# Cross-attention without key projections: queries taken through the transposed key weights, scored on the context in blocks of 125 rows

## The chip, the cores and the metric

The kernel runs on 1 core of one Trainium2 chip. The metric is the device time of one execution in microseconds, as the median of several runs.

## The reference, cut to what matters

`x` is (8, 100, 512), the context (8, 361, 512), all float32. A single-head attention adds 0.1 of its result to `x`. After it come two layers of 16-head cross-attention (128 columns a head) with a layer norm ahead of each, and an MLP (512 to 2048 to 512) with its own norm.

```python
qh = (q_in @ wq + bq).reshape(b, q_len, H, K)
kh = (kv_in @ wk + bk).reshape(b, t, H, K)
vh = (kv_in @ wv + bv).reshape(b, t, H, K)
kh = jnp.concatenate([kh, jnp.broadcast_to(bias_k, (b, 1, H, K))], axis=1)
vh = jnp.concatenate([vh, jnp.broadcast_to(bias_v, (b, 1, H, K))], axis=1)
logits = jnp.einsum('bqhk,bthk->bhqt', qh, kh) / scale
weights = jax.nn.softmax(logits, axis=-1)
ctx = jnp.einsum('bhqt,bthk->bqhk', weights, vh).reshape(b, q_len, H * K)
return ctx @ wo + bo
```

## The kernel before

**Precision.** Nearly every float32 matrix is held as a high part and a low part, the rest after rounding. A product is three matmuls (high by high, high by low, low by high; `mm3`, lines L466 to L468), and over 512 contracted rows (`product`) twelve. ScalarE makes the high part of each result out of PSUM, VectorE the low part behind it (`low` L978, `low_biased` L982), so that each result goes TensorE, ScalarE, VectorE and back.

**Stages.** The single-head stage (`single_head` on each engine) handles the 8 batches in two turns of four. Its VectorE order is in `batches`, and `residual` (L1047) ends a turn. Then, for each half of the batches (4 batches, 400 query rows), come two layers and the MLP, in loops of the program (`Fori`). `x_ready` is raised at the end of each block: by the `flag` memset (L986) after the single head and after each layer, by the copy of `x_next` (L1288) after an MLP. I call one layer on one half a pass; there are four. A normalisation begins each pass and each MLP (`norm_sums`, `norm_act`, `norm_dve`); it needs `norm_p`, which SP loads as its first act after `x_ready`.

**A pass** goes over 8 pairs of heads, 8 steps a pair, one for each batch and head (`pair_steps`). A step projects the keys of one head and batch (`keys`, 12 matmuls of 362 columns: the 361 context rows and one column for `bias_k`), scores 100 queries on them (`scores_at`, 3 matmuls), takes the softmax (`maxima`, `exps`, `normalise`), transposes the probabilities (`prob_rows`, L594) and, every second step, attends for both heads at once over the context rows (`attend`, 36 matmuls of 200 columns). The values' weights are applied after the attention (`outputs_part`, with L624 for the biases), then the output weights (`project`). Two key projections run inside the normalisation:

```python
norm_sums(half * 6 + l * 2, lambda: keys(0, 0, True))
keys(0, 1, True)
pe.wait_ge(n_lo, half * 6 + l * 2 + 2)
```

**Weights** come by SP in pieces of 512 KB (two heads of one kind, `load`, L259) into two stage buffers, and GpSimd splits them (`split_one`: copy L339, subtraction L361, for each head).

## Time and profile before

| | us |
|---|---|
| median of 3 runs | 2142.31 (2141.86 to 2143.52) |
| span of the profiled execution | 2136.5 |
| median less this span | 5.8 |
| TensorE busy | 1999.7 (94%) |
| VectorE busy | 1478.8 (69%) |
| ScalarE busy | 765.9 (36%) |
| GpSimd busy | 746.6 (35%) |

The profiled execution has no time of its own beside its span; the span is from its first to its last instruction. Busy time is the union of an engine's instructions. Matmuls overlap in the records, so the pace of a row of them is read from the difference of two starts, not from the length of one.

### The profile page before, as it was taken

What the parts mean: (1) busy time and instruction counts of PE and PEld (TensorE: products, weight loads), DVE (VectorE), ACT (ScalarE), POOL (GpSimd) and SP (SyncE); (2) the same over time, 40 slices, a digit from 0 to 9 for tenths busy, and PEclk for the clock granted to TensorE, in tenths of its full rate; (3) what the DMA queues carried; (4) which work ended last, traced back from release to release, by engine and by line L of the source; (5) the groups of instructions that cost most, each with busy time, mean ns of one, the idle gap of its engine ahead of it and who ended that gap; (6) DMA issues with size and microseconds to landing.
All of it is one profiled execution on the core that took longest, in us unless ns stands there. A gap on an engine that the chain in (4) does not pass through costs nothing.

```text
span 2136.5 us, 38048 instructions
## 1 busy us (share of the span) xinstructions
PE 1999.7 (94%) x13128; PEld 1944.5 (91%) x13128; DVE 1478.8 (69%) x3365; ACT 765.9 (36%) x1723; POOL 746.6 (35%) x609
## 2 busy tenths in 40 slices
PE   7779999999889999999797999999979999999978
PEld 4679999999879999999696999999979999999968
DVE  3456777777567777777667677777766777777677
ACT  3433333333233333333453333333333333333354
POOL 2223333333313333333361333333323333333355
PEclk9999999999999999999898999999989999999989
DMA  7401111111001111111432011111101111111054
GB/s 222 137 20 51 40 39 39 39 39 40 21 31 40 39 39 39 41 49 38 140 117 74 31 40 39 39 39 41 47 23 40 47 42 39 39 39 40 21 170 130
DMA packets 37685, 119.84 MB, mean 56 GB/s; under 512 B 5168, under 2 KB 6320, under 8 KB 37600
## 3 DMA queue, kind: packets, MB, share of 16 engines
q1 hardware_dynamic: 35296, 114.52, 16.6%
q10 hardware_dynamic: 2304, 4.20, 0.6%
q8 instruction: 52, 0.85, 0.2%
q14 instruction: 33, 0.27, 0.0%
HBM read 116.24 MB, written 2.46 MB: 56 GB/s over the span
## 4 chain that ended last, share of the span: by engine, by line
PE 84%; DVE 7%; issue 4%; ACT 3%; DMA 1%; POOL 1%; SPq 0%; DVEq 0%; ACTq 0%; POOLq 0%
PE psum L466 26%; PE psum L467 26%; PE psum L468 26%; PE psum L594 3%; PE psum L482 1%; DMA cr_stage<-ctx_dram 1%; DVE rstd L1096 1%; DVE prob L998 1%; PE psum L624 1%; DVE xT L1178 1%; DVE stats L990 1%; DVE xT L1276 0%; DVE cen L1100 0%; DVE u_lo L978 0%; DVE pT_lo L978 0%
## 5 line engine op out<-in xcount | busy, mean ns | idle before, releaser
L466 PE MATMUL psum<-pT_hi,ctx_rows_hi 121*128 121x200 f32 (+1 forms) x1536 | 425.1, 277 | 15.4 <-DVE pT_lo L978 10.5
L467 PE MATMUL psum<-pT_lo,ctx_rows_hi 121*128 121x200 f32 (+1 forms) x1536 | 426.3, 278 | 0.0
L468 PE MATMUL psum<-pT_hi,ctx_rows_lo 121*128 121x200 f32 (+1 forms) x1536 | 424.4, 276 | 0.0
L855 ACT ACTIVATE prob<-psum,stats 100x362 f32<-100x362 f32 x256 | 144.4, 564 | 631.8 <-DVE stats L992 631.8
L466 PE MATMUL psum<-ctxT_hi,wk_hi 128*128 128x362 f32 x1024 | 336.9, 329 | 0.0
L467 PE MATMUL psum<-ctxT_lo,wk_hi 128*128 128x362 f32 x1024 | 335.5, 328 | 0.0
L468 PE MATMUL psum<-ctxT_hi,wk_lo 128*128 128x362 f32 x1024 | 335.5, 328 | 0.0
L339 POOL TENSOR_TENSOR wo_hi<-stage,zero_col 128x512 fp32r<-128x512 f32 x60 | 62.4, 1041 | 770.0 <-PE psum L468 660.3
L466 PEld LDWEIGHTS psum<-pT_hi,ctx_rows_hi 121*128 121x128 f32 (+1 forms) x1536 | 297.3, 194 | 24.5 <-issue 12.0
L468 PEld LDWEIGHTS psum<-pT_hi,ctx_rows_lo 121*128 121x128 f32 (+1 forms) x1536 | 298.2, 194 | 0.0
L467 PEld LDWEIGHTS psum<-pT_lo,ctx_rows_hi 121*128 121x128 f32 (+1 forms) x1536 | 296.0, 193 | 0.0
L978 DVE TENSOR_TENSOR u_lo<-psum,u_hi 128x400 fp32r<-128x400 f32 x256 | 141.6, 572 | 103.2 <-ACT u_hi L738 102.2
L466 PEld LDWEIGHTS psum<-ctxT_hi,wk_hi 128*128 128x128 f32 x1024 | 193.3, 189 | 0.6
L467 PEld LDWEIGHTS psum<-ctxT_lo,wk_hi 128*128 128x128 f32 x1024 | 193.0, 189 | 0.0
L468 PEld LDWEIGHTS psum<-ctxT_hi,wk_lo 128*128 128x128 f32 x1024 | 192.8, 188 | 0.0
L738 ACT ACTIVATE u_hi<-psum 128x400 fp32r<-128x400 f32 x256 | 126.1, 504 | 164.7 <-PE psum L468 164.7
L996 DVE RECIPROCAL stats<-stats 100x1 f32<-100x1 f32 x264 | 43.3, 164 | 190.2 <-ACT prob L855 184.4
L738 ACT ACTIVATE pT_hi<-psum 121x300 fp32r<-121x300 f32 x256 | 106.9, 418 | 177.2 <-PE psum L594 176.7
L978 DVE TENSOR_TENSOR pT_lo<-psum,pT_hi 121x300 fp32r<-121x300 f32 x256 | 117.9, 460 | 67.1 <-ACT pT_hi L738 67.1
L998 DVE TENSOR_SCALAR prob<-prob,stats 100x362 f32<-100x362 f32 (+1 forms) x264 | 153.7, 582 | 9.2
L982 DVE SCALAR_TENSOR_TENSOR k_lo<-psum,bk_c,k_hi 128x361 fp32r<-128x361 f32 x256 | 150.2, 587 | 3.0 <-ACT k_hi L844 0.7
L990 DVE TENSOR_REDUCE stats<-psum 100x1 f32<-100x362 f32 (+1 forms) x264 | 139.7, 529 | 12.8 <-PE psum L468 8.9
(176 smaller groups left out, 4687.2 us busy)
## 6 DMA issues: line engine op xcount, KB each, us to landing
stage<-pair_w_dram SPq DMA_DIRECT2D x130, 512.0 KB, 3.7
stage<-mlp_w_dram SPq DMA_DIRECT2D x32, 512.0 KB, 3.7
ct_stage<-ctxT_dram SPq DMA_DIRECT2D x16, 722.0 KB, 4.4
cr_stage<-ctx_dram SPq DMA_DIRECT2D x32, 240.0 KB
l0w<-l_w_dram ACTq DMA_DIRECT2D x16, 256.0 KB, 12.9
cr_stage<-ctx_dram SPq DMA_DIRECT2D x16, 242.0 KB
x_next<-out_dram SPq DMA_DIRECT2D x2, 800.0 KB, 5.6
out_dram<-y_out SPq DMA_DIRECT2D x8, 200.0 KB, 2.0
```

Of the source, the lines that this page charges most:

```text
L339: return nc.gpsimd.tensor_tensor(out, in_, zero_col[0:in_.shape[0], :].broadcast_to(tuple(in_.shape)), ALU.add)
L466: pe.matmul(out, w_hi, x_hi, start=start, stop=False)
L467: pe.matmul(out, w_hi, x_lo, start=False, stop=False)
L468: return pe.matmul(out, w_lo, x_hi, start=False, stop=stop)
L594: mm = pe.transpose(bank[PT_BANK][0:rows, t * L:(t + 1) * L], prob[0:L, t0:t0 + rows], ident[0:L, 0:L])
L738: return nc.scalar.activation(out, in_, ACT.Copy)
L855: nc.scalar.activation(prob[0:L, :], bank[S_BANK][0:L, 0:T], ACT.Exp, bias=stat[:, 1:2], scale=HEAD_SCALE, accum_out=stat[:, 2:3]).then_in ...
L978: return nc.vector.tensor_tensor(out, value, hi.bitcast(F32), sub)
L982: return nc.vector.scalar_tensor_tensor(out=out, in0=value, scalar=bias, in1=hi.bitcast(F32), op0=ALU.add, op1=sub)
L990: nc.vector.reduce_max(st[:, 0:1], scores, AX_X).then_inc(max_s, 1)
L996: nc.vector.reciprocal(st[:, 3:4], st[:, 2:3]).then_inc(rcp_s, 1)
L998: nc.vector.tensor_scalar(p, p, st[:, 3:4], None, ALU.mult).then_inc(norm_s, 1)
```

## The change

- There are no projected keys. A head's query result goes through the head's transposed key weights (`through_keys`, 4 results of 3 matmuls, 400 columns), which gives 512 numbers for each query, and these are scored on the split context itself (`scores`, 12 matmuls of 362 columns for one block and batch). The key bias cancels in the softmax except against the `bias_k` column. That column's scores come from a product of their own at the start of a pass (16 rows, 400 columns), go to DRAM and come back as columns (`s0_d`, three reads of 4 numbers a run), and VectorE copies one column into the scores before the maximum.
- The weights of that product are made at run time: for each of the 32 heads of both layers a 0.5 KB row is spread over 128 partitions and a 256 KB piece of `wq` is loaded (`load_key_weights`), GpSimd multiplies (`key_weights`), VectorE sums (`key_sums`). VectorE does 24 of the 32 sums inside turn 1 of the single head, six after each batch, and 8 after its last residual; then come two more operations and `x_ready`.
- All 16 heads of a batch form one row of 1600 queries, cut in 12 blocks of 125 and one of 100. Two blocks are attended together (250 columns, `attend`), the last three together (350 columns). A step is such a group on one batch: 24 steps a pass, 52 blocks in place of 64.
- The order of queries, key products, values and outputs is the table `PIECES`; they share three PSUM banks in turn (`RBUFS`). Queries and their products live in a ring of five heads (`a`).
- Weights come one head at a time (256 KB) through two stage buffers to four weight buffers. SP issues the first six of a pass ahead of `norm_p`.
- The loops are written out. Contexts 2 and 3 of the second use are loaded at the end of the first MLP, and the second MLP neither reloads contexts nor copies `x_next`.

```diff
+BLK = 125
+SLOTS = 5
+RING = SLOTS * L
+BLOCKS = [(j * BLK, min(BLK, H * L - j * BLK)) for j in range(-(-H * L // BLK))]
+UNITS = [(0, 1), (2, 3), (4, 5), (6, 7), (8, 9), (10, 11, 12)]
+WIDE = 350
+PT_STEP = BLK + 1
+STEPS = [(k, b) for k in range(len(UNITS)) for b in range(NB)]
+LATE = (2, 4)
+PIECES = {
+    "start": "q0 q1 k0 q2 k1",
+    (0, 0, "a"): "k2", (0, 1, "b"): "q3", (0, 2, "a"): "k3", (0, 2, "b"): "q4", (0, 3, "a"): "k4",
+    (1, 0, "b"): "v0 v1", (1, 1, "a"): "o0", (1, 1, "b"): "q5 o1", (1, 2, "a"): "k5", (1, 2, "b"): "q6",
+    (1, 3, "a"): "k6",
+    (2, 0, "b"): "v2 v3 o2 v4 q7 o3 k7 o4", (2, 1, "b"): "q8", (2, 2, "a"): "k8", (2, 2, "b"): "q9", (2, 3, "a"): "k9",
+    (3, 0, "b"): "v5 v6", (3, 1, "a"): "o5", (3, 1, "b"): "q10 o6", (3, 2, "a"): "k10", (3, 2, "b"): "q11",
+    (3, 3, "a"): "k11",
+    (4, 0, "b"): "v7 v8 o7 v9 q12 o8 k12 o9", (4, 1, "b"): "q13", (4, 2, "a"): "k13", (4, 2, "b"): "q14",
+    (4, 3, "a"): "k14",
+    (5, 0, "b"): "v10 v11 o10 q15 o11 k15",
+    "end": "v12 v13 o12 v14 o13 v15 o14 o15",
+}
+PLACES = ["start"] + [(k, b, place) for k, b in STEPS for place in "ab"] + ["end"]
+KINDS = "qkvo"
+def pieces(place):
+    return [(word[0], int(word[1:])) for word in PIECES.get(place, "").split()]
+ORDER = [piece for place in PLACES for piece in pieces(place)]
...
+            def load_key_weights(i):
+                wait(sp, kw_s, i - 1)
+                sp.dma_start(kb[:, i % 2, :], diff_d[i, 0].partition_broadcast(P)).then_inc(kb_ld[i % 2], 16)
+                load_stage(i, head_w_d[i * 4 + KINDS.index("q")])
...
+            def load_weights(ph, i):
+                kind, h = ORDER[i]
+                if ph * W_LAYER + i < STAGES:
+                    sp.wait_ge(kw_s, LAYERS * H)
+                else:
+                    sp.wait_ge(stage_free, ph * W_LAYER + i - STAGES + 1)
+                load_stage(LOADS_BEFORE + ph * W_LAYER + i, head_w_d[((ph % LAYERS) * H + h) * 4 + KINDS.index(kind)])
...
+                    early = WBUFS + STAGES
+                    if l == 0:
+                        for i in range(early):
+                            load_weights(ph, i)
+                    load_norm(half, l)
+                    sp.wait_ge(s0_row, ph + 1)
+                    wait(sp, s_col, ph * S_LAYER)
+                    sp.dma_start(s0_d.rearrange("(h n) -> h n", n=N), s0_rows[:, :]).then_inc(s0_out, 16)
+                    sp.wait_ge(s0_out, ph * 16 + 16)
+                    whole = len(BLOCKS) - 1
+                    rows0 = s0_d[0:whole * BLK * NB].rearrange("(j p b) -> p j b", p=BLK, b=NB)
+                    rows1 = s0_d[whole * BLK * NB:H * N].rearrange("(p b) -> p b", b=NB)
+                    sp.dma_start(s0_cols[0:112, 0:whole, :], rows0[0:112]).then_inc(s0_ld, 16)
+                    sp.dma_start(s0_cols[112:BLK, 0:whole, :], rows0[112:BLK]).then_inc(s0_ld, 16)
+                    sp.dma_start(s0_cols[0:BLOCKS[whole][1], whole, :], rows1).then_inc(s0_ld, 16)
...
+            def key_weights(i):
+                pool.wait_ge(kb_ld[i % 2], i // 2 * 16 + 16)
+                pool.wait_ge(stage_ld[i % STAGES], i // STAGES * 16 + 16)
+                wait(pool, kw_sum, i - 1)
+                nc.gpsimd.tensor_tensor(kw[:, i % 2, :, :], stage[i % STAGES][:, :].rearrange("p (c k) -> p c k", k=P),
+                                        kb[:, i % 2, :].unsqueeze(1).broadcast_to((P, DC, P)), ALU.mult).then_inc(kw_s, 1)
...
+            def split_weights(ph, i):
+                use = LOADS_BEFORE + ph * W_LAYER + i
+                held = stage[use % STAGES][:, :]
+                hi, lo = w_hi[i % WBUFS][:, :], w_lo[i % WBUFS][:, :]
+                pool.wait_ge(stage_ld[use % STAGES], use // STAGES * 16 + 16)
+                if i >= WBUFS:
+                    user = ORDER[i - WBUFS]
+                    pool.wait_ge(y_mm, ph * R_LAYER + R_AT[user] + OUTPUTS[user[0]])
+                elif ph > 0:
+                    pool.wait_ge(y_mm, ph * R_LAYER)
+                copy(hi, held).then_inc(w_hi_s, 1)
+                pool.wait_ge(w_hi_s, ph * W_LAYER + i + 1)
+                nc.gpsimd.tensor_tensor(lo, held, hi.bitcast(F32), ALU.subtract).then_inc(stage_free, 1)
...
-                def keys(pair, i, first):
-                    pg = ph * PAIRS + pair
-                    b, u = divmod(i, 2)
-                    ctx_b = slice(b * T, (b + 1) * T)
-                    if b == 0:
-                        pe.wait_ge(wk_done, pg * 2 + (u + 1))
-                    wait(pe, k_lo_s, pg * STEPS, i, first)
-                    product(bank[K_BANK][:, 0:T], lambda c: chunk(wk_hi[:, u, :], c), lambda c: chunk(wk_lo[:, u, :], c),
-                            lambda c: c_hi[:, c, ctx_b], lambda c: c_lo[:, c, ctx_b]).then_inc(k_mm, 1)
...
-                def scores_at(pg, i, first):
-                    b, u = divmod(i, 2)
-                    pe.wait_ge(k_lo_s, pg * STEPS + (i + 1))
-                    if b == 0:
-                        pe.wait_ge(kcol_lo, pg * 2 + (u + 1))
-                        pe.wait_ge(q_lo_s, pg * 2 + (u + 1))
-                    wait(pe, s_exp, pg * STEPS, i, first)
-                    mm3(bank[S_BANK][0:L, 0:T], q_hi[:, u, batch(b)], q_lo[:, u, batch(b)],
-                        k_hi[:, u, :], k_lo[:, u, :]).then_inc(s_mm, 1)
...
+                def through_keys(h):
+                    hi, lo = weights("k", h)
+                    pe.wait_ge(y_done, ph * R_LAYER + R_AT["q", h] + 1)
+                    for m in range(DC):
+                        mm3(output("k", h, m), chunk(hi, m), chunk(lo, m), a_hi[:, DC - 1, :, slot(h)],
+                            a_lo[:, DC - 1, :, slot(h)]).then_inc(y_mm, 1)
...
+                def scores(k, b, x):
+                    i = S_AT[k, b, x]
+                    f0, rows = BLOCKS[UNITS[k][x]]
+                    last_head = (f0 + rows - 1) // L
+                    pe.wait_ge(y_done, ph * R_LAYER + R_AT["k", last_head] + DC)
+                    wait(pe, s_exp, ph * S_LAYER + i - 1)
+                    ctx_b = slice(b * T, (b + 1) * T)
+                    product(bank[S_BANK + i % 2][0:rows, 0:T], lambda c: a_hi[:, c, b, ring(f0, rows)],
+                            lambda c: a_lo[:, c, b, ring(f0, rows)], lambda c: c_hi[:, c, ctx_b],
+                            lambda c: c_lo[:, c, ctx_b]).then_inc(s_mm, 1)
...
+                before = None
+                for k, b in STEPS:
+                    scores(k, b, 0)
+                    if before is not None:
+                        turn_probs(*before, len(UNITS[before[0]]) - 1)
+                    run_pieces((k, b, "a"))
+                    late = k in LATE and b == 0
+                    if not late:
+                        scores(k, b, 1)
+                    if before is not None:
+                        attend(*before)
+                    if late:
+                        run_pieces((k, b, "b"))
+                        scores(k, b, 1)
+                    turn_probs(k, b, 0)
+                    if not late:
+                        run_pieces((k, b, "b"))
+                    if len(UNITS[k]) == 3:
+                        scores(k, b, 2)
+                        turn_probs(k, b, 1)
+                    before = k, b
+                turn_probs(*before, len(UNITS[before[0]]) - 1)
+                attend(*before)
+                run_pieces("end")
+
+            def mlp_block(half):
...
+                def beside_second(b):
+                    if b == 0:
+                        split_ctx_lo(3, 7)
+                    for _ in range(6):
+                        key_sums(next(keys))
...
+                batches(1, beside_second)
+                dve.wait_ge(landed, 16)
+                residual(1, x1)
+                for i in keys:
+                    key_sums(i)
+                key_parts()
...
+                def maxima(k, b, x):
+                    j = UNITS[k][x]
+                    i = S_AT[k, b, x]
+                    rows = BLOCKS[j][1]
+                    dve.wait_ge(s_mm, ph * S_LAYER + i + 1)
+                    scored = bank[S_BANK + i % 2][0:rows, 0:T]
+                    nc.vector.tensor_copy(scored[:, 0:1], s0_cols[0:rows, j, b:b + 1]).then_inc(s_col, 1)
+                    dve.wait_ge(s_col, ph * S_LAYER + i + 1)
+                    nc.vector.tensor_reduce(stats[0:rows, i % 2, 0:1], scored, AX_X, ALU.max, negate=True).then_inc(s_max, 1)
```

**VectorE in turn 1 of the single head** (`p` are the probabilities, `kw` the multiplied weights). Before:

```order
L978 TENSOR_TENSOR ctxT_lo<-ct_stage,ctxT_hi 128x4x361
L978 TENSOR_TENSOR p_lo<-psum,p_hi 121x300
L990 TENSOR_REDUCE stats<-psum 100x1
L992 TENSOR_SCALAR stats<-stats 100x1
L996 RECIPROCAL stats<-stats 100x1
L998 TENSOR_SCALAR prob<-prob,stats 100x361
L978 TENSOR_TENSOR h_lo<-psum,h_hi 128x4x100
```

Now:

```order
L992 TENSOR_TENSOR ctxT_lo<-ct_stage,ctxT_hi 128x4x361
L1015 TENSOR_REDUCE w<-kw 128x4 x6
L992 TENSOR_TENSOR p_lo<-psum,p_hi 121x300
L1029 TENSOR_REDUCE stats<-psum 100x1
L1031 TENSOR_SCALAR stats<-stats 100x1
L1035 RECIPROCAL stats<-stats 100x1
L1037 TENSOR_SCALAR prob<-prob,stats 100x361
L992 TENSOR_TENSOR h_lo<-psum,h_hi 128x4x100
L1015 TENSOR_REDUCE w<-kw 128x4 x6
```

Six sums now stand between the low part of the context and the low part of the next batch's probabilities, and six after each later batch.

**SP at the start of the first pass** (`stage` are the weights, `s` is the scores' first column). Before:

```order
L255 DMA out_dram<-xT 128x1600 [waits y_add]
L259 DMA stage<-pair_w_dram 128x1024 [waits lq_mm]
L259 DMA stage<-pair_w_dram 128x1024 [waits wq_done]
...
L274 DMA norm_p<-norm_p_dram 128x12
```

Now:

```order
L277 DMA stage<-head_w_dram 128x512 [waits kw_s] x2
L277 DMA stage<-head_w_dram 128x512 [waits stage_free] x4
L321 DMA norm_p<-norm_p_dram 128x12 [waits x_ready]
L333 DMA s_scratch<-s_rows 16x400 [waits s0_row]
L338 DMA s_cols<-s_scratch 112x12x4 [waits s0_out]
L339 DMA s_cols<-s_scratch 13x12x4
L340 DMA s_cols<-s_scratch 100x4
```

Four loads that each wait for a split by GpSimd have moved ahead of `norm_p`.

**VectorE in one step of a pass, now** (`a` is the ring):

```order
L1217 TENSOR_REDUCE stats<-psum 125x1
L992 TENSOR_TENSOR pT_lo<-psum,pT_hi 121x3x125
L1224 RECIPROCAL stats<-stats 125x1
L1226 TENSOR_SCALAR prob<-prob,stats 125x362
L1240 CAST pb<-pT_lo 1x250
L992 TENSOR_TENSOR a_lo<-psum,a_hi 128x2x250 x2
```

The low parts of the probabilities of the step before come between the maximum and the normalising of the first block, and the attended results come last.

## Rows read from the trace of the kernel before

**Rows 1.** The page: span; busy time of each engine.
```profile
span 2136.5 us, 38048 instructions
...
PE 1999.7 (94%) x13128; PEld 1944.5 (91%) x13128; DVE 1478.8 (69%) x3365; ACT 765.9 (36%) x1723; POOL 746.6 (35%) x609
```

**Rows 2.** Views of two VectorE lines: ns min/median/max, first to last start in us.
```profile
L986 DVE MEMSET flag<- x5: 59/59/59, 140.6 to 2033.9; 128x1 f32 x5
...
L1288 DVE COPY xT<-x_next x2: 3682/3756/3831, 1133.3 to 2132.6; 128x1600 f32<-128x1600 f32 x2
```

**Rows 3.** View of line L624 on TensorE, 210 to 270 us.
```profile
L624 PE MATMUL psum<-pb,dv x3: 347/347/350, 216.6 to 268.8; 65*128 65x400 f32 x3
```

**Rows 4.** Timeline of TensorE, 702 to 712 us: start us, us, instruction, xcount.
```profile
702.70 0.33 PE L466 MATMUL psum<-ctxT_hi,wk_hi 128*128 128x362 f32 x1
...
704.70 0.34 PE L466 MATMUL psum<-h_hi,wq_hi 128*128 128x400 f32 x1
...
706.89 0.44 PE L594 MATMUL psum<-ident,prob 100*121 100x100 f32 x3
707.12 0.39 PE L466 MATMUL psum<-k_hi,q_hi 128*100 128x362 f32 x1
...
707.68 0.33 PE L466 MATMUL psum<-ctxT_hi,wk_hi 128*128 128x362 f32 x1
...
709.66 0.26 PE L466 MATMUL psum<-pT_hi,ctx_rows_hi 121*128 121x200 f32 x1
...
711.98 0.27 PE L466 MATMUL psum<-pT_hi,ctx_rows_hi 121*128 121x200 f32 x1
```

**Rows 5.** Timeline of TensorE, 569 to 571 us.
```profile
569.52 0.30 PE L466 MATMUL psum<-u_hi,wv_hi 128*128 128x300 f32 x1
...
570.35 0.30 PE L624 MATMUL psum<-pb,dv 65*128 65x300 f32 x1
```

**Rows 6.** Groups by line and shape: busy us, mean ns, idle before and releaser.
```profile
L466 PE MATMUL psum<-pT_hi,ctx_rows_hi 121*128 121x200 f32 x1024 | 284.1, 277 | 15.4 <-DVE pT_lo L978 10.5 <-issue 4.8
...
L466 PEld LDWEIGHTS psum<-ctxT_hi,wk_hi 128*128 128x128 f32 x1024 | 193.3, 189 | 0.6
...
L982 DVE SCALAR_TENSOR_TENSOR k_lo<-psum,bk_c,k_hi 128x361 fp32r<-128x361 f32 x256 | 150.2, 587 | 3.0 <-ACT k_hi L844 0.7 <-issue 0.2
...
L466 PEld LDWEIGHTS psum<-k_hi,q_hi 128*100 128x100 f32 x256 | 43.1, 168 | 0.0
```

**Rows 7.** Timeline of TensorE in the single-head stage, [idle before <-releaser].
```profile
61.15 0.48 PE L466 MATMUL psum<-ctx_rows_hi,p_hi 121*100 121x512 f32 x1 [1.25 <-DVE p_lo L978]
...
106.19 0.54 PE L523 MATMUL psum<-ident,prob 100*121 100x100 f32 x3 [2.14 <-DVE prob L998]
```

**Rows 8.** Timeline, first normalisation, 140 to 156 us.
```profile
144.67 2.05 DVE L1090 TENSOR_SCALAR cen<-cen,norm_p 128x200 f32<-128x200 f32 x8
...
155.76 0.67 PE L466 MATMUL psum<-h_hi,wq_hi 128*128 128x400 f32 x1 [5.32 <-DVE h_lo L982]
```

**Rows 9.** Windows of TensorE: stretch, length, busy (matmuls), granted clock, DMA share, GB/s.
```profile
156.00:160.00 4.00, 4.00 (x13) 0.51 0.00 0
```

**Rows 10.** The DMA view: queue, count, KB each, us to landing.
```profile
norm_p<-norm_p_dram SPq DMA_DIRECT2D x6, 6.0 KB, 1.6
```

**Rows 11.** Timeline of SP and of GpSimd, 92 to 141 us.
```profile
100.63 22.38 SPq L259 DMA_DIRECT2D stage<-pair_w_dram  x2
...
114.22 3.60 POOL L354 TENSOR_TENSOR ctx_rows_lo<-cr_stage,ctx_rows_hi 121x1536 fp32r<-121x1536 f32 x1 [17.07 <-ACT ctx_rows_hi L738]
...
126.29 1.04 POOL L339 TENSOR_TENSOR wk_hi<-stage,zero_col 128x512 fp32r<-128x512 f32 x1 [3.64 <-DMA stage<-pair_w_dram]
127.41 1.26 POOL L361 TENSOR_TENSOR wk_lo<-stage,wk_hi 128x512 fp32r<-128x512 f32 x1
```

**Rows 12.** Timeline of GpSimd and of SP, 40 to 92 us.
```profile
60.36 3.58 POOL L354 TENSOR_TENSOR ctx_rows_lo<-cr_stage,ctx_rows_hi 121x1536 fp32r<-121x1536 f32 x1 [15.62 <-ACT ctx_rows_hi L738]
...
60.64 0.35 SPq L234 DMA_DIRECT2D ct_stage<-ctxT_dram  x1
```

More of the change, by code:

```diff
@@ new lines, in project, with run_pieces @@
+                def project(h):
+                    hi, lo = weights("o", h)
+                    pe.wait_ge(y_done, ph * R_LAYER + R_AT["v", h] + 1)
+                    for m in range(DC):
+                        mm3(output("o", h, m), chunk(hi, m), chunk(lo, m), a_hi[:, 0, :, slot(h)], a_lo[:, 0, :, slot(h)])\
+                            .then_inc(y_mm, 1)
+                def run_pieces(place):
+                    for kind, h in pieces(place):
+                        {"q": queries, "k": through_keys, "v": values, "o": project}[kind](h)
@@ L728, in _ @@
             single_head()
-            with pe.Fori(0, HALVES) as half:
-                with pe.Fori(0, LAYERS) as l:
+            key_bias()
+            for half in range(HALVES):
+                for l in range(LAYERS):
                     layer(half, l)
@@ L1239, in layer @@
[L1239 to L1248 removed]
+                norm_dve(norm_at(half, l), half * 3 + l)
@@ new lines, in add_output, with run_pieces @@
+                def add_output(h):
+                    for m in range(DC):
+                        n = ph * R_LAYER + R_AT["o", h] + m
+                        dve.wait_ge(y_mm, n + 1)
+                        nc.vector.tensor_tensor(columns(xT[:, m, :]), made("o", h, m), columns(xT[:, m, :]), ALU.add)\
+                            .then_inc(y_done, 1)
+                def run_pieces(place):
+                    for kind, h in pieces(place):
+                        if kind == "v" and h % 2 == 0:
+                            bias_rows(h // 2)
+                        {"q": queries_lo, "k": through_keys_lo, "v": values_lo, "o": add_output}[kind](h)
@@ L1296, in _ @@
             dve.wait_ge(mlp_b_ld, 16)
-            with dve.Fori(0, HALVES) as half:
-                with dve.Fori(0, LAYERS) as l:
+            for half in range(HALVES):
+                for l in range(LAYERS):
                     layer(half, l)
```

1190 lines of the change are left out of this document (564 added, 626 removed).

## The prediction

> **What bounds the kernel now.** I read the page first: TensorE is busy for 1999.7 of 2136.5 us [rows 1], so the kernel is paced by its matmuls, and a change pays by taking matmul time off TensorE without opening waits. The milestones cut the span into stages [rows 2]: `x_ready` first rises at 140.6 (end of the single head) and for the last time by that memset at 2033.9. The first MLP ends with the copy at 1133.3 plus 3.8, at 1137.1. So two passes take 2033.9 - 1137.1 = 896.8, one pass 448.4, and the two MLPs get 2136.5 - 140.6 - 4 x 448.4 = 202.3.
>
> Inside a pass the same matmul of two pairs lies 268.8 - 216.6 = 52.2 apart [rows 3]; 8 pairs are 417. The other 31 us of a pass are its normalisation (15.2 from `x_ready` to the first query matmul at 155.76 [rows 2, 8], with 4 us of keys inside) and its tail.
>
> The pace of a matmul comes from starts [rows 4]. Twelve key matmuls of 362 columns take 704.70 - 702.70 = 2.00 (0.167 each). Twelve of 400 columns take 706.89 - 704.70 = 2.19 (0.182). A group of transposes takes 0.23, three score matmuls 0.56. Of 200 columns 21 take 2.32 (0.110). Of 300 columns six take 0.83 (0.138) [rows 5]. Narrow matmuls are thus dear for each column: 200 to 300 costs 0.028, 300 to 362 another 0.029.
>
> **Part 1, TensorE's work in a pass.** Removed: keys 64 x 2.00 = 128.0, scores 64 x 0.56 = 35.8, transposes 64 x 0.23 = 14.7, attending 1152 x 0.110 = 127; together 305.5. Queries, values and outputs stay (32 x 2.19 and 16 x 2.37 = 108). Added: products with the transposed keys 16 x 2.19 = 35.0; scores 52 x 2.06 = 107 (2.00 and the slower first matmul of a score); transposes 52 x 0.25 = 13 (125 columns; between 0.23 and 0.29 by columns). Attending is 720 matmuls of 250 columns and 144 of 350. For 250 no row stands; it lies between 0.110 and 0.138, and I take 0.120, nearer to the line through 300 and 362 (0.115) than to the middle. 350 lies just under 362, 0.161. That is 86.4 + 23.2 = 109.6. The `bias_k` product is 12 matmuls right after an idle stretch; in such a place the granted clock was 0.51, the 1.2 GHz level, with 13 matmuls in 4.0 us [rows 9]: 4 us. Added: 268.6. **Work: -37 a pass.**
>
> The weights of the score matmuls now have 125 columns. Loads of 100 columns took 168 ns in the records against 189 for 128 [rows 6], and the 362-column matmuls behind them kept the pace, so I add nothing. The Trainium skill (TensorE: Matmul & The Clock Gate, Weight-path perf modes) says that the fast weight load is on only where the number of weights is 128 and the type isn't FP32. By that rule the new scores would lose it; the rows with 100 columns show no loss, and the rivals price it.
>
> **Part 2, the rest of a pass.** Before, it is 448.4 - 413.5 of work = 35. After it is the normalisation and the waits.
>
> *Normalisation.* `norm_p` is needed by the scaling operations at 144.67, 4.1 after `x_ready` [rows 8], and lands 1.6 after issue [rows 10]. Now it stands behind six weight loads on SP, and the sixth waits for four splits by GpSimd, which in a later pass start with the last matmul of the pass before. A split is 1.04 + 1.26 and a gap, 2.45 [rows 11], so four end some 10 us later, `norm_p` is there 11.4 after `x_ready`, and TensorE starts 9.9 behind it (2.05 of scaling; the chain from there to 155.76 took 9.0, of which a key split goes): 21.3. In the first pass the loads wait for the last key weight and GpSimd also clears two tiles: 25.5. The keys that filled 4 us here are gone; nothing covers this.
>
> *Waits.* (a) The start of a pass has three places where TensorE uses a result just made, at about 1.5 each (ScalarE and VectorE about 0.6 each [rows 6] and gaps): 4.5. (b) Three banks for the four key results: the fourth waits about 0.3, 16 times: 5. (c) The last group has a third block close behind: 2.4 four times less cover, and a key product just before its scores: 4. (d) The end has a bare softmax chain (2.14) and a bare split of the probabilities (1.25) [rows 7]: 3.5. (e) Values after attending: 3. (f) After idle stretches the clock falls for some 3 us, four times at 1.5: 6. Together 26, of which I know only (d) from rows like it; 12 to 45.
>
> *A middle step.* TensorE has 2.0 + 0.25 + 2.0 + 5.8 + 0.25 = 10.3, VectorE about 6.2 (two blocks at 0.8 maximum, 0.75 normalising, 0.55 split; two attended results at 0.68; the row copy). The tightest cover: the split of the first block's probabilities must end before the second's transposes. It ends 2.05 after the attending, and these start 2.27 after. I cost it at nothing; if it is missed, see rival D. The trip of the `bias_k` scores through DRAM (ScalarE 0.6, write 2, read 3 or more) runs beside five products and the first scores, 15 us; nothing.
>
> Pass after: 376.6 of work + 21.3 + 26 = 423.9, and 4 more in the first. **Four passes: 1700 against 1794, -94.**
>
> **Part 3, the single head.** In turn 0 SP now waits for GpSimd's key difference, which runs behind its context split that ends at 63.94, then for a write to land, about 2, where it sent the context load at 60.64 [rows 12]: turn 1 comes 6.5 later. In turn 1 GpSimd's last context split ended at 117.8 [rows 11], now 124.3, and then come the 32 key weights. For each, SP issues two loads (0.35 each [rows 12]). A load of 512 KB issued at 122.65 was used at 126.29, 3.64 [rows 11]; one of 6 KB lands in 1.6 [rows 10]; 256 KB lies between, I take 2.6. The multiplication costs 1.2. Two are in flight: (0.45 + 2.6 + 0.05 + 1.2) / 2 = **2.15 a key**, at least 1.3 (GpSimd alone), at most 2.7 by 3.64. VectorE waits for 24 of them in its order, with the next batch's probabilities behind it and TensorE behind these. 24 are done at 124.3 + 1.3 + 23 x 2.15 = 175. Then the last 48 products and residuals, 13: 188.5. GpSimd is only two ahead, so six more need 1.3 + 1.3 + two rounds of 4.3, with the sums: 201, and `x_ready` comes at **202 against 140.6, +61**.
>
> **Part 4, the MLPs.** The first has context loads 2 and 3 at its very end, one behind the other (+8, less 4 of waits that the middle loses). The second loses a 1.3 us memset, context work and the last copy of 3.8, of which the output's landing leaves 1.5: -10. 202.3 becomes 196.
>
> **Sum.** 202 + 1700 + 196 = 2098 against a span of 2136.5, -38.5. The median of the runs is 5.8 above that span, and I add the same: **2104**.
>
> **The rivals.**
> - **B, lighter ends (0.20).** If key weights go at GpSimd's 1.3, 25 us go; waits of 15 instead of 26 a pass take 44 more: 2035. For it: eight times 64 KB need only 2 us more than 6 KB [rows 10, 11]. Against it: there are only two stage buffers, and waits (a) to (d) are in the written order.
> - **C, slower: key weights one after the other (0.12).** If a load starts only when the one before is used, a key costs 4.3, the single head gains 32 x 2.15 = 69 more: 2173. It turns the sign from 3.35 a key on. Against: two buffers and two semaphores each.
> - **D, slower: the softmax chain shows in each step (0.13).** One bare microsecond in each of 96 steps gives 2200; 0.4 a step uses up the gain. For: the slack of 0.2 above. Against: before, pairs ran with about 0.5 of wait in 52.
> - **E, slower: the weight loads of 125 columns set the pace (0.05).** At 0.19 each [rows 6] in place of 0.167, the 2496 score matmuls give +57: 2161. This is what the rule of the Trainium skill above would amount to here.
> - **F, it cancels out (0.05).** Some of each lands within 2138 to 2147.
> - That the change doesn't do what it says: the written order shows 2496 matmuls of 362 columns for the scores and no key projection, so I give it nothing.
>
> **How the numbers follow.** The forecast has 0.45: 2104, its own range 2075 to 2130. About 0.2% is what a measurement tells from no change. C, D and E hold 0.30, of which 0.05 is milder than their turning points and still faster. Faster: 0.45 + 0.20 + 0.05 = 0.70. Slower: 0.25. Same (F): 0.05. The range takes B's near half, and D and C up to 2165: 2050 to 2165.
>
> **What would show it.** Right: `x_ready` first near 202 with six sums of VectorE spaced at 2.15; passes near 424; 250-column matmuls 0.12 apart, scores 0.167; 10 or more us of idle TensorE ahead of each pass's first product, ended by the low part of `h`, with `norm_p` issued late. Wrong: a first `x_ready` beyond 230 (C), an idle TensorE before each group of transposes (D), scores 0.19 apart (E), or a pass above 445.

## The result

| | before | changed |
|---|---|---|
| median | 2142.91 us | 2276.45 us (2275.35 to 2277.14) |
| ratio | | 1.062 (95%: 1.061 to 1.064) |
| span of the profiled execution | 2136.5 us | 2274.7 us |
| first `x_ready` | 140.6 | 211.5 |
| the four passes | 448.3, 446.3, 449.4, 447.3 | 468.5, 464.2, 469.5, 464.2 |
| first MLP | 102.0 | 104.1 |
| from the last `x_ready` to the end | 102.6 | 92.8 |

The change makes the kernel 6.2% slower. 2104 was forecast, with a range of 2050 to 2165. Times without a unit are microseconds. The MLPs came out near their term and the single head 9.5 us late; each pass is 40 to 46 us longer than forecast.

### The profile page after: what moved, and what is told of

It is laid out like the page before. It is cut to its first block, busy times and chain, and to the rows that moved or that the text cites. A ratio compares the mean times of both kernels' runs of the same rounds, so it can differ in the third digit from the quotient of the medians.

```text
span 2274.7 us, 30085 instructions
## 1 busy us (share of the span) xinstructions
PE 1915.0 (84%) x11204; PEld 1800.2 (79%) x11204; DVE 1239.0 (54%) x2623; ACT 806.9 (35%) x1832; POOL 768.0 (34%) x634
## 4 chain that ended last, share of the span: by engine, by line
PE 70%; DVE 13%; ACT 6%; DMA 4%; issue 4%; POOL 3%; SPq 0%; DVEq 0%; ACTq 0%; POOLq 0%
PE psum L474 23%; PE psum L476 21%; PE psum L475 21%; PE psum L654 3%; DMA stage<-head_w_dram 2%; DVE a_lo L1001 2%; DVE pT_lo L992 2%; ACT pT_hi L737 1%; DVE a_lo L996 1%; PE psum L490 1%; DVE dv L1163 1%; POOL kw L404 1%; DVE xT L1200 1%; POOL ctx_rows_lo L388 1%; ACT a_hi L861 1%
## 5 line engine op out<-in xcount | busy, mean ns | idle before, releaser
L474 PE MATMUL psum<-a_hi,wbuf_hi 128*128 128x400 f32 x768 | 304.5, 396 | 110.2 <-DVE dv L992 89.3
L474 PE MATMUL psum<-pT_hi,ctx_rows_hi 121*128 121x250 f32 (+3 forms) x1152 | 337.4, 293 | 13.3 <-DVE pT_lo L992 13.3
L419 POOL TENSOR_TENSOR wbuf_lo<-stage,wbuf_hi 128x512 fp32r<-128x512 f32 x256 | 330.2, 1290 | 20.0
L476 PE MATMUL psum<-pT_hi,ctx_rows_lo 121*128 121x250 f32 (+3 forms) x1152 | 333.1, 289 | 0.0
L475 PE MATMUL psum<-pT_lo,ctx_rows_hi 121*128 121x250 f32 (+3 forms) x1152 | 329.1, 286 | 0.0
L474 PE MATMUL psum<-ctxT_hi,a_hi 128*125 128x362 f32 (+1 forms) x832 | 282.8, 340 | 15.2 <-DVE a_lo L1001 15.2
L475 PE MATMUL psum<-a_lo,wbuf_hi 128*128 128x400 f32 x768 | 282.0, 367 | 0.0
L476 PE MATMUL psum<-a_hi,wbuf_lo 128*128 128x400 f32 x768 | 281.2, 366 | 0.0
L475 PE MATMUL psum<-ctxT_lo,a_hi 128*125 128x362 f32 (+1 forms) x832 | 274.2, 330 | 0.0
L476 PE MATMUL psum<-ctxT_hi,a_lo 128*125 128x362 f32 (+1 forms) x832 | 273.7, 329 | 0.0
L992 DVE TENSOR_TENSOR a_lo<-psum,a_hi 128x500 fp32r<-128x500 f32 (+2 forms) x288 | 145.9, 525 | 193.7 <-ACT a_hi L737 192.9
```

The source lines that it names most:

```text
L419: nc.gpsimd.tensor_tensor(lo, held, hi.bitcast(F32), ALU.subtract).then_inc(stage_free, 1)
L474: pe.matmul(out, a_h, x_hi, start=start, stop=False)
L475: pe.matmul(out, a_h, x_lo, start=False, stop=False)
L476: return pe.matmul(out, a_l, x_hi, start=False, stop=stop)
L992: return nc.vector.tensor_tensor(out, value, hi.bitcast(F32), sub)
```

## The profile after

The page (answers to [rows 1]):

```profile
span 2274.7 us, 30085 instructions
...
PE 1915.0 (84%) x11204; PEld 1800.2 (79%) x11204; DVE 1239.0 (54%) x2623; ACT 806.9 (35%) x1832; POOL 768.0 (34%) x634
```

The view of the `flag` memset (answers to [rows 2]): ns min/median/max, first to last start.

```profile
L1005 DVE MEMSET flag<- x5: 59/59/59, 211.5 to 2181.9; 128x1 f32 x5
```

TensorE did lose 85 us of busy time, and VectorE 240. What grew is the time in which TensorE stands still. The matmuls themselves behave as forecast. Timeline of TensorE in a middle step, 760 to 768 us (answers to [rows 4]):

```profile
760.61 0.28 PE L474 MATMUL psum<-pT_hi,ctx_rows_hi 121*128 121x250 f32 x1
...
763.40 0.28 PE L474 MATMUL psum<-pT_hi,ctx_rows_hi 120*128 120x250 f32 x1
...
763.75 0.48 PE L654 MATMUL psum<-ident,prob 125*121 125x125 f32 x3
763.99 0.41 PE L474 MATMUL psum<-ctxT_hi,a_hi 128*125 128x362 f32 x1
...
766.06 0.48 PE L654 MATMUL psum<-ident,prob 125*121 125x125 f32 x3
```

24 matmuls of 250 columns take 763.40 - 760.61 = 2.79 us, 0.116 each (forecast 0.120). A block's scores take 766.06 - 763.99 = 2.07 (2.06), its transposes 0.24 (0.25).

The waits of TensorE in pass 2 from its first product on, 703 to 1145 us (what it waited for: us, times, longest):

```profile
PE psum L474 <- DVE dv L992: 22.3, 8, 3.3
PE psum L654 <- DVE prob L1226: 4.7, 4, 2.7
PE psum L474 <- DVE a_lo L1001: 4.1, 4, 1.5
PE psum L474 <- DVE pT_lo L992: 3.3, 3, 1.2
PE psum L474 <- DVE a_lo L996: 3.2, 12, 0.3
```

The last four add to 15.3, close to the 17 that the prediction put down for (a) to (d): the start, the three banks, the last group, the end. Two of the three `pT_lo` waits (2.3 us) are of a kind it didn't name: they come ahead of the attending in the two steps of a pass whose second block is scored late (`LATE`). The first row it did not name either, and it is more than all the others. `dv` are the rows of the value bias. For each pair of heads VectorE casts a row of 256 numbers twice and subtracts once (L1162, L1163, L992), just ahead of the pair's value product, where TensorE waits for it. VectorE, GpSimd and TensorE at the second pair of pass 2:

```profile
842.88 1.04 POOL L373 TENSOR_TENSOR wbuf_hi<-stage,zero_col 128x512 fp32r<-128x512 f32 x1 [0.30 <-PE psum L476]
843.26 0.80 DVE L1162 CAST dv<-dv 1x256 fp32r<-1x256 f32 x1
844.00 1.26 POOL L419 TENSOR_TENSOR wbuf_lo<-stage,wbuf_hi 128x512 fp32r<-128x512 f32 x1
844.08 1.33 DVE L1163 CAST dv<-dv 1x256 fp32r<-1x256 f32 x1
845.44 0.42 DVE L992 TENSOR_TENSOR dv<-dv 1x256 fp32r<-1x256 f32 x1
...
845.91 0.70 PE L474 MATMUL psum<-a_hi,wbuf_hi 128*128 128x400 f32 x1 [3.18 <-DVE dv L992]
...
846.41 0.54 PE L475 MATMUL psum<-a_lo,wbuf_hi 128*128 128x400 f32 x1
846.75 0.54 PE L476 MATMUL psum<-a_hi,wbuf_lo 128*128 128x400 f32 x1
```

Three things are to be seen. The chain of three is on the path. Each cast ends 0.15 us behind the GpSimd operation beside it (844.06 and 843.92, 845.41 and 845.26), so the two did not run side by side. And after the wait the matmuls of 400 columns start 0.34 apart instead of 0.18.

At four of the eight pairs GpSimd is idle, the three operations take 1.07 together, and TensorE still stands for 2.2 to 2.5. The first pair of pass 2 shows the rest (TensorE and VectorE):

```profile
772.56 0.48 PE L654 MATMUL psum<-ident,prob 125*121 125x125 f32 x3
...
773.38 0.68 DVE L992 TENSOR_TENSOR a_lo<-psum,a_hi 128x500 fp32r<-128x500 f32 x1 [1.41 <-ACT a_hi L737]
773.98 0.54 DVE L992 TENSOR_TENSOR pT_lo<-psum,pT_hi 121x375 fp32r<-121x375 f32 x1
774.43 0.27 DVE L1162 CAST dv<-dv 1x256 fp32r<-1x256 f32 x1
...
775.50 0.45 PE L474 MATMUL psum<-a_hi,wbuf_hi 128*128 128x400 f32 x1 [2.46 <-DVE dv L992]
```

VectorE makes the rows last, so to wait for them is to wait also for the second attended result and for the low part of the probabilities. The value product needs the first of these only halfway through, and the second not at all. At the other four pairs, beside GpSimd, the waits are 3.2 to 3.3: GpSimd's share of the 22.3 is some 3.5 us, by the difference of the two kinds.

The operations are not new. The view of tile `dv` of the kernel before (ns min/median/max):

```profile
L1140 DVE CAST dv<-dv x32: 280/281/284, 211.4 to 2010.4; 1x256 fp32r<-1x256 f32 x32
L1141 DVE CAST dv<-dv x32: 282/283/285, 211.7 to 2010.7; 1x256 fp32r<-1x256 f32 x32
```

The same view of the changed kernel:

```profile
L1162 DVE CAST dv<-dv x32: 270/272/871, 309.9 to 2164.9; 1x256 fp32r<-1x256 f32 x32
L1163 DVE CAST dv<-dv x32: 282/768/1329, 310.2 to 2165.8; 1x256 fp32r<-1x256 f32 x32
```

Before, no wait of TensorE ended with them, and none was slower than another. Windows of the changed kernel (stretch, length, busy and count of PE, PEld, DVE, ACT, POOL; granted clock; DMA share, GB/s) show the clock behind two such waits, which end at 845.91 and 914.12:

```profile
846.00:850.00 4.00, 4.00 (x12) 3.96 (x13) 0.00 (x0) 0.00 (x0) 0.00 (x0) 0.50 0.21 66
915.00:919.00 4.00, 4.00 (x14) 3.95 (x13) 0.00 (x0) 0.15 (x1) 0.04 (x1) 0.50 0.13 47
```

After a stop of some 3 us TensorE works for 4 us and more at half clock (1.2 of 2.4 GHz): 12 and 14 matmuls in 4 us.

**The sum of one pass.** The gap between the starts of every two matmuls of pass 2 is set against the usual gap after a matmul of that kind. The usual gaps add to 368.7 us. What lies above them is 59.0 where TensorE stopped and 14.6 where the clock was low. That is 442.3; with 22.0 from `x_ready` to the first product it is 464.3. The same sum for a pass of before is 412.7, 11.3 and 5.1.

## The experiments

All are edits of the changed kernel. Times are medians, ratios are to the kernel before on the same chip, whose own medians there were 2143.6 (e1 to e4), 2145.0 (e5 to e8) and 2143.5 (e9 to e11).

### e1: no bias rows

SP's load, VectorE's `bias_rows` and TensorE's wait are gone. The rows stay zero, so this kernel leaves out the part of the values that they carry.

```diff
-                    pe.wait_ge(dv_lo_s, ph * (H // 2) + h // 2 + 1)
...
-                        if kind == "v" and h % 2 == 0:
-                            bias_rows(h // 2)
```

> The changed kernel without the making and loading of the bias rows: the rows stay zero, so the bias_v part of the values is left out. Theory A (late bias rows): a pass of the changed kernel has 59 us of waits and 15 us of slow clock around 369 us of matmuls; eight waits for the rows hold 23 us of it and call forth most of the clock falls after them, so a pass should fall by 28 to 34 us and the kernel by 110 to 135, to 2140 to 2165. Rival B (hand-over through ScalarE and VectorE: three shared PSUM banks, results used just after they are made): TensorE would meet the results' own latency at the same places, the waits only change their name, and at most 10 us a pass go: 2235 or more.

Measured: **2138.8 us**, ratio 0.998 (0.997 to 0.999): 138 less than the changed kernel and 1 below the range of theory A. Three short operations, 32 times, bound up with a wait, are worth as much as the whole loss against before. In pass 2 the first value product now starts right behind the transposes, without a stop:

```profile
736.59 0.48 PE L653 MATMUL psum<-ident,prob 125*121 125x125 f32 x3
736.83 0.43 PE L472 MATMUL psum<-a_hi,wbuf_hi 128*128 128x400 f32 x1
```

### e3: the rows one pair ahead

Two buffers; VectorE makes a pair's rows behind the value product of the pair before. All work is done.

```diff
-        dv3 = sb("dv3", [65, 2 * P], F32R)
+        dv3 = sb("dv3", [65, 2, 2 * P], F32R)
...
-                        if kind == "v" and h % 2 == 0:
-                            bias_rows(h // 2)
+                        if kind == "v" and h % 2 == 0 and h // 2 + 1 < H // 2:
+                            bias_rows(h // 2 + 1)
```

> The changed kernel with two buffers for the bias rows, each pair's rows made one pair earlier. All work is done. Theory A: as without the rows, less the VectorE time of the three small operations, which now run beside matmuls: 2145 to 2170. Rival B: 2235 or more. Third possibility: the operations on one partition (up to 1.3 us beside GpSimd) now delay the results behind them on VectorE, and 5 to 10 us a pass come back: 2170 to 2200.

Measured: **2142.5 us**, ratio 1.000 (0.999 to 1.001), within 4 us of leaving the rows out, and just under theory A's range. The casts are still slow, and it costs nothing (view of tile `dv`):

```profile
L1164 DVE CAST dv<-dv x32: 282/781/1362, 252.7 to 2028.7; 1x256 fp32r<-1x256 f32 x32
```

So it is the wait that costs, not the operations. The sum of pass 2 is now 368.7 + 36.1 of stops + 4.4 of low clock: 22.9 and 10.2 less.

### e5: TensorE waits where it needs the rows

VectorE's order is left alone. Only the last of a value product's thirteen matmuls reads the rows.

```diff
-                    pe.wait_ge(dv_lo_s, ph * (H // 2) + h // 2 + 1)
...
+                    pe.wait_ge(dv_lo_s, ph * (H // 2) + h // 2 + 1)
                     pe.matmul(out, dv3[:, h % 2 * P:(h % 2 + 1) * P], pb3[:, :, slot(h)], start=False, stop=True)\
```

> One line moved on TensorE's side alone: in a value product TensorE waits for the bias rows ahead of the one matmul that reads them, and no longer ahead of all thirteen. VectorE makes them where the changed kernel does. Theory A (TensorE stood still for 2.8 us eight times a pass because it waited too early): twelve matmuls of 0.182 us, 2.2 us, now cover the wait, some 0.6 us of each of the 32 waits stays, and with them go the falls of the clock: 2150 to 2175 us. Theory B (VectorE is late in itself, and what comes behind the rows on VectorE holds TensorE as well): the waits move to the next results, and the time stays above 2220.

Measured: **2164.2 us**, ratio 1.009 (1.007 to 1.010). One moved line gives back 112 of the 134 us. Half of the waits are left, at most 1.2 us long:

```profile
PE psum L621 <- DVE dv L992: 17.1, 16, 1.2
```

They stand at the four pairs of a pass at which GpSimd runs. Theory B falls: VectorE is not late with anything else there.

### e6: the same wait, with TensorE busy in it

Ahead of each of the 32 waits stand twelve more matmuls. They write a result that the value product then overwrites.

```diff
+                    if h % 2 == 0:
+                        product(out, lambda c: chunk(hi, c), lambda c: chunk(lo, c), lambda c: h_hi[:, c, :],
+                                lambda c: h_lo[:, c, :])
                     pe.wait_ge(dv_lo_s, ph * (H // 2) + h // 2 + 1)
```

> The changed kernel with twelve more matmuls of 400 columns ahead of each wait for the bias rows, 32 times; their result is overwritten, so nothing of the computation is left out. The wait stays; only TensorE is busy in it. 12 x 0.182 = 2.2 us against waits of 2.3 to 3.3 us. Theory A (after each stop the clock is lower for some matmuls, 14.6 us a pass where two of the norm's and the end's remain): 8 to 10 us a pass come back: 2235 to 2250 us. Theory B (the fall of the clock belongs to other places, or costs nothing beside the wait): 2270 to 2285 us.

Measured: **2234.8 us**, ratio 1.042 (1.040 to 1.044). 384 more matmuls make the kernel 42 us faster. Up to 1.2 us of each stop is left. In pass 2 the waits behind which the clock stood at 0.50 before end at 833.29 and 899.04 in this kernel:

```profile
834.00:838.00 4.00, 4.00 (x24) 4.00 (x23) 0.63 (x1) 0.60 (x1) 1.85 (x2) 1.00 0.18 61
900.00:904.00 4.00, 4.00 (x26) 4.00 (x25) 0.90 (x3) 0.60 (x1) 2.10 (x2) 1.00 0.10 38
```

The clock's share of the loss is thus some 40 us, as the sum of a pass has it (4 x 10.2), and the stops themselves take the other 92 (4 x 22.9).

### e11: half of the rows earlier, with one buffer

```diff
+AHEAD = (0, 1, 5, 6)
...
+                    for kind, h in pieces((k, b, "b")):
+                        if kind == "v" and h // 2 in AHEAD and h % 2 == 0:
+                            bias_rows(h // 2)
                     if before is not None:
                         attended_lo(*before)
```

> The changed kernel with its one buffer of bias rows; VectorE makes the rows of pairs 0, 1, 5 and 6 ahead of the attended results instead of behind them. Those of pairs 2, 3, 4 and 7 can't go there, because the value product that frees the one buffer comes after these results. Theory A (the place in VectorE's order makes the wait): in pass 2 the four moved waits are 2.3 to 2.5 us long, they go with their falls of the clock, some 13 us a pass: 2215 to 2235 us. Theory B (VectorE has no time free there either, and the attended results come later by as much): above 2260 us.

Measured: **2224.0 us**, ratio 1.038 (1.036 to 1.040). 16 waits are left (before them it was 32 times, 89.3 us):

```profile
PE psum L475 <- DVE dv L993: 52.2, 16, 3.4
```

This is in theory A's range. Four of the eight waits come from the place in VectorE's order alone; there VectorE had idle time ahead of the attended results (1.41 us ahead of the one at 773.38 above). The other four come from the single buffer, which is free only when the value product ahead has run. These are also the four at which GpSimd runs.

### e10: the rows by another operation

```diff
-                    nc.vector.tensor_copy(dv3[0:1, :], row)
-                    nc.vector.tensor_copy(dv3[32:33, :], row).then_inc(dv_hi_s, 1)
+                    zero = zero_col[0:1, 0:1].broadcast_to((1, 2 * P))
+                    nc.vector.tensor_tensor(dv3[0:1, :], row, zero, ALU.add)
+                    nc.vector.tensor_tensor(dv3[32:33, :], row, zero, ALU.add).then_inc(dv_hi_s, 1)
```

> The changed kernel, its two copies of a bias row (1x256, 0.27 us alone, 0.8 to 1.33 us beside GpSimd's subtraction, at four of eight pairs) written as additions of a zero column. The last operation of the three, a subtraction of two tiles, kept its 0.416 us in all 32 places. Theory A (only the copying form is slow beside GpSimd): additions cost some 0.13 us more each where GpSimd is idle and 0.4 to 0.9 less where it isn't: 3 us less a pass, 2260 to 2267 us. Theory B (an addition stands still too, and the subtraction kept its time only because GpSimd was done by then): 2274 to 2285 us.

Measured: **2289.0 us**, ratio 1.068 (1.066 to 1.069), 12.6 more than the changed kernel and 4 above what theory B gave. Additions stand still beside GpSimd too, which is theory B's form; and they cost 0.13 us more each where it is idle (0.40 for the first, 0.41 for the second below):

```profile
L1164 DVE TENSOR_TENSOR dv<-dv,zero_col x32: 414/901/1390, 310.1 to 2177.6; 1x256 fp32r<-1x256 f32 x32
```

The subtraction that ends the three is no exception: it kept its 0.42 here, where GpSimd is done by then, and in e3, where it lies beside a split at some pairs, it takes up to 1.31.

### e2 and e7: `norm_p` early, and GpSimd held back

e2 loads the norm's parameters as soon as the norm before has used them, in place of behind six weight loads. e7 adds a wait of GpSimd ahead of a pass's first split.

```diff
-            def load_norm(half, l):
-                sp.wait_ge(x_ready, x_is(half, l))
+            def load_norm(done, l):
+                sp.wait_ge(n_res, done)
...
+                if i == 0:
+                    pool.wait_ge(n_lo, norm_at(ph // LAYERS, ph % LAYERS) + 1)
```

> The changed kernel with norm_p loaded as soon as the normalisation before has used it, ahead of the weight loads. Theory: norm_p is what VectorE waits for, 8 to 9.5 us in each of four passes, so 34 us go and a little more by the clock: 2235 to 2245. Rival: the splits by GpSimd then run beside the normalisation and slow VectorE on its way (seen as operations of 1.3 in place of 0.3 us), and half of the gain or less is left: 2255 to 2265.

Measured: **2253.7 us**, ratio 1.052 (1.049 to 1.054), 22.7 less: between the two ranges, 1 below the rival's. The timeline says why. The norm of pass 2 in the changed kernel (SP, VectorE, TensorE):

```profile
689.65 0.43 SPq L321 DMA_DIRECT2D norm_p<-norm_p_dram  x1
...
692.12 1.96 DVE L1129 TENSOR_SCALAR cen<-cen,norm_p 128x200 f32<-128x200 f32 x8 [8.05 <-DMA norm_p<-norm_p_dram]
...
701.97 0.51 PE L474 MATMUL psum<-h_hi,w_hi 128*16 128x400 f32 x1 [15.32 <-DVE h_lo L996]
```

And in e2 (VectorE, TensorE):

```profile
676.48 5.62 DVE L1130 TENSOR_SCALAR cen<-cen,norm_p 128x200 f32<-128x200 f32 x8
...
689.99 0.52 PE L475 MATMUL psum<-h_hi,w_hi 128*16 128x400 f32 x1 [10.85 <-DVE h_lo L997]
```

The wait of 8.05 us for `norm_p` is gone (over the four passes it was 8.0 to 9.5). But the eight scaling operations, 1.96 us alone, now lie beside GpSimd's splits and take 5.62: of 8.05 us, 3.66 are given back.

> e2 again (norm_p loaded ahead), and GpSimd starts a pass's first weight split only when the first half of the low part of h is made. In e2 the eight scaling operations took 5.62 us beside GpSimd's splits where they took 1.96 us without them. Theory A (the two engines slow each other): the scaling takes 2 us again, the passes' normalisation gets 3.6 us shorter, four times: 2236 to 2244 us against 2253.7. Theory B (the weights of the first query are then late by as much): 2250 to 2262 us.

Measured: **2255.0 us**, ratio 1.051 (1.049 to 1.053), no gain over e2. Theory A was right on the scaling and missed the total; theory B had the total, by a cause that is not there (the first query's weights were not waited for). VectorE in e7, pass 2:

```profile
676.63 2.05 DVE L1132 TENSOR_SCALAR cen<-cen,norm_p 128x200 f32<-128x200 f32 x8
...
683.41 1.43 DVE L999 SCALAR_TENSOR_TENSOR h_lo<-cen,norm_p,h_hi 128x200 fp32r<-128x200 f32 x4
685.08 4.96 DVE L999 SCALAR_TENSOR_TENSOR h_lo<-cen,norm_p,h_hi 128x200 fp32r<-128x200 f32 x4 [0.23 <-ACT h_hi L829]
```

The splits now start at 684.97 and slow the second low part, 4.96 against 1.43. The 3.6 us moved to a later operation of the same chain.

### e4: the weights of the `bias_k` scores by TensorE

For each head TensorE multiplies `wq`, stored the other way round, by one column (4 matmuls of one column); the spread rows, GpSimd's products and VectorE's sums are gone. The context loads of turn 1 also no longer wait for the write of the key difference, so the gain in `x_ready` is of both together.

```diff
-                nc.gpsimd.tensor_tensor(kw[:, i % 2, :, :], stage[i % STAGES][:, :].rearrange("p (c k) -> p c k", k=P),
...
+            def key_products(i):
+                pe.wait_ge(kq_ld[i % 4], i // 4 * 16 + 16)
+                for c in range(DC):
+                    at = c * LAYERS * H + i
+                    mm = pe.matmul(bank[3][:, at:at + 1], chunk(kq[i % 4], c), k_diff[:, i:i + 1])
```

> The changed kernel with the weights of the bias_k product made on TensorE (one-column float32 matmuls with transposed query weights from DRAM, four buffers) in place of 32 rounds of spreading, multiplying and summing. Theory C (the ladder of loads, GpSimd and VectorE holds the single head at 211.5 us): x_ready comes at 142 to 155 us, and the first normalisation is a few us longer for the last 12 weights; 2215 to 2230. Rival: the 8 MB of loads themselves bound it (256 KB each in some 1.3 us at best, beside the contexts), and only half is gained: x_ready near 175, 2240 to 2250.

Measured: **2257.4 us**, ratio 1.052 (1.049 to 1.055): 19 less, where 46 to 61 or 26 to 36 were expected. `x_ready` came at 167.2, 44.3 earlier, but the first pass took 496.2 in place of 468.5. The waits of TensorE from 160 to 230 us in e4:

```profile
PE psum L466 <- DVE w_lo L999: 29.2, 1, 29.2
```

The timeline of SP and of VectorE in that time:

```profile
190.25 14.76 SPq L278 DMA_DIRECT2D stage<-head_w_dram  x6
205.06 0.42 SPq L322 DMA_DIRECT2D norm_p<-norm_p_dram  x1
...
207.59 1.96 DVE L1126 TENSOR_SCALAR cen<-cen,norm_p 128x200 f32<-128x200 f32 x8 [36.30 <-DMA norm_p<-norm_p_dram]
```

`norm_p` again: it stands behind six weight loads, and these waited for the last key weight. Both theories had left that queue out, and `x_ready` at 167.2 lies between them.

### e8 and e9: the repairs together

e8 is e2, e3 and e4 in one kernel. e9 is e8 with GpSimd's first split of a pass held until both halves of the low part are made (`+ 2` in e7's wait).

> e2, e3 and e4 in one kernel: bias rows one pair ahead, norm_p loaded early, the weights of the bias_k scores made by TensorE. Theory A (the three are independent, and e4 lost its 44 us in the first pass only because norm_p stood behind weight loads that waited for the last key weight, 29.2 us of TensorE's time): first x_ready at 165 to 168 us, no such wait, first pass near 435: 2080 to 2095 us. Theory B (the first pass waits for the key weights anyway): the first pass stays 25 us longer than the others, 2105 to 2120 us.

Measured: **2084.4 us**, ratio 0.972 (0.970 to 0.974). First `x_ready` 167.5, first pass 436.6, the others 426.5, 429.3, 426.5: theory A. With the early `norm_p` the 29 us of e4 are gone.

> e8, and GpSimd starts a pass's first weight split when both halves of the low part of h are made. In e7 it started after the first half: the scaling took 2.05 us instead of 5.62, but the second half of the low part took 4.96 us instead of 1.44, and nothing was won. Theory A (whatever VectorE does beside the splits there is slow, and the four splits can run beside the bias_k product of 4 us and the first queries): 3.6 us less in each of four passes, 2068 to 2075 us against 2084.4. Theory B (the first query's weights are then too late): 2082 to 2090 us.

Measured: **2075.1 us**, ratio 0.968 (0.966 to 0.969): 3.2% faster than the kernel before. 9 of the 14 us of theory A came, at the upper end of its range; the later passes got 3.0 to 3.7 shorter, the first none. The norm of pass 2 in e9, VectorE and GpSimd:

```profile
610.27 2.05 DVE L1130 TENSOR_SCALAR cen<-cen,norm_p 128x200 f32<-128x200 f32 x8
...
618.72 1.44 DVE L1007 SCALAR_TENSOR_TENSOR h_lo<-cen,norm_p,h_hi 128x200 fp32r<-128x200 f32 x4 [0.23 <-ACT h_hi L837]
620.08 4.02 DVE L1147 TENSOR_SCALAR xT<-xT,norm_p 128x400 f32<-128x400 f32 x4
...
620.29 1.10 POOL L376 TENSOR_TENSOR wbuf_hi<-stage,zero_col 128x512 fp32r<-128x512 f32 x1 [22.17 <-DVE h_lo L1007]
```

The splits slow only the operation on the residual (4.02, alone 1.44), for which nothing waits there.

## Why the prediction was wrong

The span came out 177 above the forecast sum of 2098, and 166 of it lie in the four passes: forecast 1700, measured 1866. The rest is near: single head 211.5 against 202, MLPs 196.9 against 196. (The median lies 1.8 above this span; I had added 5.8.) No rival's price reached this time, and of the signs of being wrong it was the last that came, a pass above 445. For pass 2:

| | forecast | measured |
|---|---|---|
| matmul work | 376.6 | 368.7 |
| `x_ready` to first product | 21.3 | 22.0 |
| stops (a) to (e) | 20 | 59.0 |
| low clock (f) | 6 | 14.6 |

- **The failed step is (e), "Values after attending: 3".** It priced TensorE's wait for the attended results and left out that VectorE makes the bias rows between these and the value product, with TensorE's wait ahead of the whole product. That wait takes in all that VectorE has in its order up to the rows. It measured 22.3 us a pass in the waits view, 22.9 between starts (e3). The three operations stand nowhere in the prediction; in the kernel before they had another place in the order and no wait of TensorE ended with them. The chain could have been priced from operations that the trace of before does show, though none of its rows was among those I had chosen.
- **(f), the clock, was mis-sized with it.** Of the 14.6 us of pass 2, 10.2 go when the rows are ahead (e3), and the whole kernel wins 42 when the stops are filled (e6). 4.4 remain, under the 6 that I priced for four places. The mechanism was there; eight more stops were not.
- **GpSimd as a neighbour was not in the prediction at all.** It makes 0.28 us into up to 1.33 at four of eight pairs. I had counted only its queue and its pace. The trace of before already showed it, in the copy of 3.8 us of [rows 2], which the prediction takes for the copy's own length (GpSimd and VectorE, before):

```profile
1132.91 3.42 POOL L354 TENSOR_TENSOR ctx_rows_lo<-cr_stage,ctx_rows_hi 121x1536 fp32r<-121x1536 f32 x1 [7.99 <-ACT ctx_rows_hi L738]
1133.35 3.83 DVE L1288 COPY xT<-x_next 128x1600 f32<-128x1600 f32 x1
```

  In the changed kernel the same copy starts 0.8 ahead of GpSimd's subtraction and takes 0.99.
- **The other stops were under-priced.** With the rows ahead (e3) 36.1 are left where (a) to (d) gave 17. The rows of the waits view for them add to 17.4 in e3's pass 2, near the forecast; but between starts twice as much is missing, in some 80 places of over 0.1 us each. Part of it is that a row counts from the end of a matmul's record (0.34 after its start) and the next would have started at 0.18. How the rest divides stays open.
- **Part 2's normalisation was right**, 22.0 against 21.3, by the cause given: `norm_p` issued 9.7 after `x_ready`, landed 2.4 later (1.6 was taken), TensorE 9.85 behind the start of the scaling. In the first pass it was 25.9 against 25.5; the third took 25.9 too, which the sum did not have.
- **Part 1 was right**, 368.7 of work against 376.6. The 250-column pace was 0.116, nearer to the line through 300 and 362 columns than I took. Rival E and the rule of the Trainium skill behind it (TensorE: Matmul & The Clock Gate, Weight-path perf modes) did not show: the groups by shape give loads of 125 columns a mean of 188 ns, and a block's scores took 2.07 as forecast.
- **Part 3 had the mechanism and a size too small.** The 24 sums inside turn 1 started from 124.7 to 183.7, 2.57 us a key and not 2.15, so that the last ended at 184.4 in place of 175. That is the nine microseconds. The term at fault is the landing: I took 2.6 for the piece of `wq`, and between 124 and 211 us it landed 3.4 after its issue; the sum of the prediction gives 2.55 a key with it. (The median of all 288 such loads of the kernel is 2.7.) The spread row, issued 0.36 earlier, took 3.1 and was there before it.
- **Rivals.** D had the form nearest to what came, a VectorE chain bare to TensorE, but at the probabilities of each step; those waits add to 18.7 us in 16 places of the whole kernel. B, C, E and F did not occur.

Put together: without the rows' wait the kernel stands at 2142.5, with a span of 2140.2 (e3) against the forecast sum of 2098. Those 42 us are 7 of the single head (209.1), 1 of the MLPs and 34 of the passes (1734.2), where the other stops cost more and the work less. So the failed step, worth 134 us, decides between a loss of 6.2% and a tie; it does not bring the forecast gain of 38, which went in these other terms.

## What to carry to other kernels

Write down, for each place where TensorE waits, every operation that its partner has in its order since the last thing TensorE waited for, also the short ones; a wait for three of some 0.3 us, at eight places of a pass, cost 33 us a pass. Put a wait at the first instruction that reads the data, not at the head of the product (112 us here, one line), and count a stop at its length plus the slow matmuls after it. And look along an issue queue whenever a small load is moved behind big ones: it may wait for whatever they wait for.

## What the runs showed of the hardware

- VectorE and GpSimd did not run side by side where both read SBUF: 0.27 us became up to 1.36 for a row on a single partition, eight scalings 1.96 became 5.62, four low parts 1.43 became 4.96. Casts, additions, scalings and three-operand forms were all slowed; the slowed casts ended just behind a GpSimd operation. The Trainium skill (Trainium Architecture — The Big Picture, What this means for kernel authors) says that the two share a port pair, held as an exclusive lock and not split; the two casts that end 0.15 us behind GpSimd's operations agree. An operation that reads its first operand from PSUM kept its time beside a split in e9 (0.63 us from 626.82 on, GpSimd busy from 626.63).
- Stops of 2.2 to 3.3 us brought the granted clock to 0.50 behind them, for 3.4 to 6.8 us, at seven of the eight pairs of pass 2; behind the stop of 2.46 us that ends at 1043.39 it stayed at 1.00. Twelve useless matmuls in each stop kept it at 1.00 at all eight and won 42 us (e6); the stops left there are at most 1.2.
- The same small load of `norm_p` held VectorE's scaling for 8.0 to 9.5 us in each pass, and TensorE for 29 us in one pass of e4, by its place in SP's queue. Loaded early, it gave back 22.7 us in all (e2), and the 29 (e8).
